# Flamingo layer pair, first attention: units of two heads on one batch instead of one head on one batch

## The reference

```python
x = x + tanh(g_xattn[0]) * xattn(layernorm(x), ctx, Wq, Wk, Wv, Wo, q_norm_w, k_norm_w)
# xattn: 32 query heads, 8 key/value heads (4 query heads each), head size 128
kv = concatenate([context, latents], axis=1)          # 512 + 256 = 768 keys per batch, 2 batches
q, k, v = latents @ Wq, kv @ Wk, kv @ Wv              # 256 queries per batch
q, k = rms_norm(q), rms_norm(k)                       # per head
probs = softmax(q @ k.T / sqrt(128))
out = (probs @ v).reshape(...) @ Wo
```

## Time and profile before

| | us |
|---|---|
| median of 3 runs (989.22 to 989.53) | 989.34 |
| the profiled execution | 990.12 |
| its span, first to last instruction | 988.3 |
| PE matmuls busy | 948.9 (96%) |
| DVE, ACT, POOL busy | 636.9, 479.9, 358.6 |

### The profile page before, as it was taken

One profiled execution on the slowest core, in us unless ns is written; L12 is line 12 of the kernel. 1 busy time (PEld: TensorE's weight loads), 2 busy tenths in 40 slices (PEclk: granted clock), 3 DMA queues, 4 the chain that ended last, 5 costly groups with the idle time before them and its releaser, 6 DMA issues. The chain is left out here.

```text
span 988.3 us, 18532 instructions
## 1 busy us (share of the span) xinstructions
PE 948.9 (96%) x6876; PEld 824.1 (83%) x6876; DVE 636.9 (64%) x1102; ACT 479.9 (49%) x937; POOL 358.6 (36%) x255
## 2 busy tenths in 40 slices
PE   4989999999999999999999999999999998999996
PEld 3969988998999899899989988998987886677755
DVE  5577547646765674576567557646754666888856
ACT  4356336534643563365356336534624612665634
POOL 3435316333341443253336317233214721080033
PEclk9999999999999999999999999999999999999999
DMA  6021203200310211032021103300006213933001
GB/s 234 1 49 49 55 1 85 55 9 1 94 53 0 74 25 49 0 85 64 0 60 36 53 0 85 73 12 4 30 15 221 85 43 123 223 73 60 2 1 43
DMA packets 40677, 55.01 MB, mean 56 GB/s; under 512 B 8640, under 2 KB 20544, under 8 KB 40640
## 3 DMA queue, kind: packets, MB, share of 16 engines
q1 hardware_dynamic: 40064, 54.49, 20.4%
q10 hardware_dynamic: 576, 0.00, 0.0%
HBM read 50.22 MB, written 4.26 MB: 55 GB/s over the span
## 5 line engine op out<-in xcount | busy, mean ns | idle before, releaser
L437 DVE TENSOR_TENSOR ptL<-tbank,ptH 128x512 fp32r<-128x512 f32 x192 | 132.3, 689 | 69.4 <-ACT ptH L306 66.8
L306 ACT ACTIVATE ptH<-tbank 128x512 fp32r<-128x512 f32 x192 | 115.7, 603 | 110.5 <-PE tbank L553 110.2
L553 PE MATMUL tbank<-ident,probs 128*128 128x128 f32 x864 | 132.5, 276 | 6.5 <-DVE ptL L437 3.3
L450 DVE TENSOR_REDUCE negmax<-score 128x1 f32<-128x768 f32 x128 | 120.5, 951 | 9.6 <-PE score L80 9.1
L327 ACT ACTIVATE probs<-score,negmax 128x768 f32<-128x768 f32 x128 | 115.7, 904 | 17.4 <-DVE negmax L450 17.3
L78 PE MATMUL obank<-ptH,vH 128*128 128x256 f32 x384 | 121.3, 316 | 0.0
L408 DVE TENSOR_REDUCE sumsq<-probs 128x2 f32<-128x256 f32 (+1 forms) x80 | 42.0, 526 | 114.9 <-ACT probs L301 71.8
L553 PEld LDWEIGHTS tbank<-ident,probs 128*128 128x128 f32 x864 | 97.5, 140 | 17.3 <-DVE ptL L437 10.3
L216 POOL TENSOR_TENSOR rnorm<-sumsq,neg_half 128x2 f32<-128x2 f32 (+1 forms) x80 | 71.4, 896 | 107.3 <-DVE sumsq L410 107.1
L80 PE MATMUL obank<-ptH,vL 128*128 128x256 f32 x384 | 108.8, 283 | 0.0
L80 PE MATMUL score<-wkvH,kvT_lo 128*128 128x256 f32 x384 | 108.7, 283 | 0.0
(11 more groups left out here) (263 smaller groups left out, 2233.7 us busy)
## 6 DMA issues: line engine op xcount, KB each, us to landing
wqo_stage<-in_wq SPq DMA_DIRECT2D x9, 1024.0 KB, 5.8
wqo_stage<-in_wo SPq DMA_DIRECT2D x8, 1024.0 KB, 7.2
factors<-r_scratch SPq DMA_DIRECT2D x32, 256.0 KB, 3.9
wkv_stage<-in_wkv SPq DMA_DIRECT2D x9, 512.0 KB, 6.6
a_qS<-q_scratch SPq DMA_DIRECT2D x24, 128.0 KB, 5.2
ctx_stage<-in_ctxT SPq DMA_DIRECT2D x2, 1024.0 KB, 12.8
kS<-k_scratch SPq DMA_DIRECT2D x32, 64.0 KB, 4.2
q_scratch<-qpart SPq DMA_DIRECT2D x16, 128.0 KB, 1.9
```

The source lines that it names most:

```text
L306: act.activation(out, tbank[c % 2][:], ACT.Copy, scale=scale).then_inc(t_hi, 1)
L437: i = dve.tensor_tensor(out, tbank[c % 2][:], f32(hi), ALU.subtract)
L450: dve.tensor_reduce(negmax[:, m:m + 1], score[m % 2][:, 0:SKV], AX.X, ALU.max, negate=True).then_inc(s_max, 1)
L553: i = pe.transpose(tbank[c % 2][:, n * P:(n + 1) * P], block_in, S.ident[:])
```

## The change

A unit w is now a pair of heads on one batch: heads 2(w // 2) and 2(w // 2)+1 on batch w % 2, four units per group. A unit has four score tiles and six chunks; a chunk is one key tile by the 512 query columns of both heads, so a V chunk is three matmuls of 512 columns into the whole `obank`. PE goes through the six chunks of a unit; behind each transposed chunk comes the V chunk that is two behind, and behind each of the first four a score tile of the next unit. `probs` has eight slots, ptH and ptL have three, the turned queries of two heads are kept, and heads 2 and 3 are turned within the second unit. Queries 0 and 1 and all four score tiles of the first unit are now made in the part between the groups (and ahead of the loop for group 0); `k_rows` and `sq` move to the second half of `probs`. `normalise_o` and the split of its result now run on two heads of one batch, and the output projection of the last group goes by batch. POOL splits Wo after score tile 5 instead of 3.

```diff
-    NP, NPT = 4, 4
+    NP, NPT = 8, 3
+    later = 4 * SKV
+    k_rows = probs_mem[:, later:later + NKT * D0].rearrange("p (t d) -> p t d", d=D0)
...
-    U, CH = 2 * GRP, 3
-    order = [("q", 0), ("k", 0), ("k", 1), ("k", 2)]
+    PAIRS, CH = GRP, KVT
+    order = [("q", 0), ("k", 0), ("q", 1), ("k", 1), ("k", 2)]
+    for w in range(PAIRS):
+        for j in range(CH):
+            if w == 1 and j < 2:
+                order.append(("q", 2 + j))
+            order.append(("p", CH * w + j))
...  # ACT
             def attend(g):
+                for w in range(PAIRS):
+                    if w == 1:
+                        hi_q(g, 2)
+                    hi_p(g, CH * w)
+                    if w == 1:
+                        hi_q(g, 3)
+                    for t in range(4):
+                        hi_p(g, CH * w + t + 1)
+                        if w + 1 < PAIRS:
+                            exp(g, 4 * w + 4 + t)
+                        if t == 1 and w:
+                            hi_o(g, w - 1)
+                    hi_p(g, CH * w + CH - 1)
+            def prepare(g):
+                for i in range(2):
+                    hi_q(g, i)
+                    hi_k(g, i)
                 exp(g, 0)
+                hi_k(g, 2)
+                for m in range(1, 4):
+                    exp(g, m)
...  # DVE
             def attend(g):
+                for w in range(PAIRS):
+                    reciprocals(g, w)
+                    if w == 1:
+                        lo_q(g, 2)
+                    lo_p(g, CH * w)
+                    for t in range(4):
+                        if w + 1 < PAIRS:
+                            maximum(g, 4 * w + 4 + t)
+                        if w == 1 and t == 0:
+                            lo_q(g, 3)
+                        lo_p(g, CH * w + t + 1)
+                        if w and t == 0:
+                            normalise_o(g, w - 1)
+                    lo_p(g, CH * w + CH - 1)
...  # PE
+            def transpose_probs(g, w, j):
                 if j == 0:
+                    pe.wait_ge(s_exp, 16 * g + 4 * w + 4)
+            def times_v(g, c):
+                w, j = c // CH, c % CH
+                if j == 0 and w >= 2:
+                    pe.wait_ge(o_normed, GRP * g + w - 1)
                 pe.wait_ge(t_lo, TC * g + at["p", c] + 1)
+                key = (w % 2) * KVT + j
+                mm3(pe, obank[w % 2][:], (vH[:, key, :], vL[:, key, :]), (ptH[:, c % NPT, :], ptL[:, c % NPT, :]),
+                    j == 0, j == CH - 1).then_inc(pe_pv, 1)
             def attend(g):
+                for w in range(PAIRS):
+                    if w == 1:
+                        transpose_q(g, 2)
+                    for j in range(CH):
+                        if w == 1 and j == 1:
+                            transpose_q(g, 3)
+                        transpose_probs(g, w, j)
+                        if CH * w + j >= 2:
+                            times_v(g, CH * w + j - 2)
+                        if j < 4 and w + 1 < PAIRS:
+                            scores(g, w + 1, j)
...  # PE, ahead of the loop
-            transpose_q(0, 0)
-            for i in range(3):
-                transpose_k(0, i)
-            scores(0, 0)
+            for t in range(2):
+                transpose_q(0, t)
+                transpose_k(0, t)
+            scores(0, 0, 0)
+            scores(0, 0, 1)
+            transpose_k(0, 2)
+            scores(0, 0, 2)
+            scores(0, 0, 3)
```

More of the change, by code:

```diff
@@ L466, in normalise_o, with lo_p @@
                                   ALU.mult).then_inc(o_normed, 1)
+            def lo_p(g, c):
+                lo(g, ("p", c), ptL[:, c % NPT, :], ptH[:, c % NPT, :])
             def attend(g):
[L469 to L485, removed]
+                for w in range(PAIRS):
[12 more added lines that the diff above has]
+                    lo_p(g, CH * w + CH - 1)
             def add_out(g, t, bank):
@@ L499, in turn @@
                 add_out(g, 0, obank[0][:])
+                lo_q(g + 1, 1)
                 lo_k(g + 1, 1)
                 add_out(g, 1, obank[1][:])
+                maximum(g + 1, 0)
                 lo_k(g + 1, 2)
-                maximum(g + 1, 0)
-                maximum(g + 1, 1)
+                for m in range(1, 4):
+                    maximum(g + 1, m)
                 add_out(g, 2, obank[0][:])
@@ L514, in _ @@
             fill_items(0, 0)
-            lo_q(0, 0)
-            for i in range(3):
+            for i in range(2):
+                lo_q(0, i)
                 lo_k(0, i)
             maximum(0, 0)
-            maximum(0, 1)
+            lo_k(0, 2)
+            for m in range(1, 4):
+                maximum(0, m)
             turns(dve, turn, last)
@@ L563, in transpose_q, with scores @@
                 transposes(g, ("q", h), [q_rows[:, t, h * D0:(h + 1) * D0] for t in range(RT)])
-            def scores(g, u, tiles=(0, 1)):
-                h, b = u // 2, u % 2
-                if b == 0 and h:
+            def scores(g, w, t):
+                hp, b, m = w // 2, w % 2, 4 * w + t
+                h = 2 * hp + t // 2
+                if b == 0:
                     pe.wait_ge(t_lo, TC * g + at["q", h] + 1)
-                if h == 0:
+                if hp == 0:
                     pe.wait_ge(t_lo, TC * g + at["k", 1 + b] + 1)
[L571 to L579, removed]
@@ L600, in attend @@
-            def attend(g):
[L602 to L610, removed]
-                    for j in range(CH):
-                        if u == U - 1:
-                            times_v(g, u - 1, j)
-                        if u or j:
-                            transpose_probs(g, u, j)
-                        if 0 < u < U - 1:
-                            times_v(g, u - 1, j)
+                if m >= 2:
+                    pe.wait_ge(s_exp, 16 * g + m - 1)
@@ new lines, in scores @@
+                q = slice(b * SQ + (m % 2) * P, b * SQ + (m % 2 + 1) * P)
+                for k0, n in ((0, 512), (512, 256)):
+                    keys = slice(b * SKV + k0, b * SKV + k0 + n)
+                    i = mm3(pe, score[m % 2][:, k0:k0 + n], (qTH[:, h % 2, q], qTL[:, h % 2, q]),
+                            (kTH[:, keys], kTL[:, keys]), True, True)
+                i.then_inc(pe_s, 1)
+            def transpose_probs(g, w, j):
+                if j == 0:
+                    pe.wait_ge(s_exp, 16 * g + 4 * w + 4)
+                transposes(g, ("p", CH * w + j),
+                           [probs[:, (4 * w + n) % NP, j * P:(j + 1) * P] for n in range(4)])
@@ L641, in turn @@
                 project_kv(g + 1)
[L642 to L648 removed]
+                for t in range(2):
+                    transpose_q(g + 1, t)
+                    transpose_k(g + 1, t)
+                    output(g, t)
+                scores(g + 1, 0, 0)
+                scores(g + 1, 0, 1)
+                transpose_k(g + 1, 2)
+                output(g, 2)
+                scores(g + 1, 0, 2)
+                scores(g + 1, 0, 3)
+                output(g, 3)
             def output_heads(t, heads):
```

81 lines of the change are left out of this document (20 added, 61 removed).

## The result

| | before | after |
|---|---|---|
| median of the runs, us | 990.61 (12 runs) | 992.68 (12 runs) |
| the profiled execution | 990.12 | 993.13 |
| its span | 988.3 | 991.2 |
| start of group 0 | 18.58 | 18.40 |
| group 0 | 83.73 | 90.82 |

The changed kernel is slower by 2.1 us: its time is 1.0027 of before, 95% interval 1.0018 to 1.0036. Forecast was 985.3, the range ended at 990.5. A group starts with its first query projection; the table goes from one such start to the next.

The account below looks back on a forecast made before the run. PE was taken to bound the eight groups, with only 1.7 us of waits in a group's attention. Terms 3.3 + 0.2 - 3.5 - 4.0 = -4.0 gave a median of 985.3 us, range 979.5 to 990.5.

Parts of the forecast that it names:

- the head's chain: Ahead of the loop: four score tiles and no chunk done at 65.7, against six and three before; 3.3 us lost.
- the head's clock: Ahead of the loop: 1.2 GHz until 56.6 as before, nothing added for the clock.
- V in 512 columns: V products: 576 matmuls of 512 columns replace 1152 of 256, at the output projection's 0.2333 us each; 4.0 us won.
- waits in the groups: PE's waits in attention: 1.1 to 1.2 us instead of 1.7; 3.5 us won over groups 1 to 7, group 0 loses 0.2.
- the second rival: Ahead of the loop: new waits keep the clock at 1.2 GHz until 65.7; 988.3 us, no change; chance 0.13.
- end of 8 for the head: Ahead of the loop: upper end of the forecast loss, 8 us, if the clock stays low.
- the first border: Between units 0 and 1: head 2's queries take a `tbank`, so PE waits 0.7 us ahead of a later chunk.
- the last unit: Last unit of a group, no scores: normalisation delays the low part and oTH; 0.4 us of waits including restarts.
- the second and third border: Between units 1 and 2, and 2 and 3: chunk 5's low part just met, normalisation caught up; 0 wait.
- the first rival: Unit borders: late normalisation on DVE makes PE wait 0.45 us at 16 borders; 7.2 us lost, 992.5; chance 0.13.
- The third rival: V products: a 512-column matmul costs 0.240 us, so nothing is won; 989.3 us, no change; chance 0.10.
- The end: Behind the last V chunk: PE has 5.6 us of output work ahead of the first matmul needing it; 0.

Follow-up runs that it names:

- experiments 1 and 2: Unread 512-column matmuls put in PE's waits ahead of the loop: 33 in the changed kernel, 989.23 us; 12 in the kernel before, 988.97 us.
- experiment 4: Changed kernel with V matmuls of 256 columns again, except the first and last pass of a unit's sum: 993.63 us, ratio 1.0036.
- experiment 9: Changed kernel with head 2's queries turned earlier, third key block and third unit's normalisation later, two k/v projections in the head's waits: 976.94 us, ratio 0.9859.

## Why the prediction was wrong

| term | forecast | measured | from |
|---|---|---|---|
| the head's chain | +3.3 | +3.9 | experiments 1 and 2, full clock |
| the head's clock | 0 | +3.2 | 4.2 after less 0.96 before |
| V in 512 columns | -4.0 | -3.3 | 17 ns by 192 chunks |
| waits in the groups | -3.3 | -0.4 | 1.86 a group to 1.78; group 0 0.4 more |
| ahead of the head, behind the groups | 0 | -0.6 | -1.1 and +0.5 in the two traces; scatter, see below |
| sum | -4.0 | +2.8 | by the spans +2.9 (988.3 to 991.2) |

- **The clock of the head is the step that failed.** The prediction kept the grant "at 1.2 GHz until 56.6 as before" and full from there. It had a row with the opposite (a wait of 2.8 us, then a grant of 0.58), and it had put three more waits of 0.7 to 2 us into the new head; it gave the second rival 0.13. The rival's mechanism came true, at another place: not until 65.7 but from 64.7, 1.0 us into the wait of 2.16, and over the chunks and score tiles that follow, which the forecast had left at their full-clock prices. Its end of 8 for the head was near the 3.9 + 3.2 measured. Experiments 1 and 2 show it by filling the waits and leaving the chain; what the stretches cost came to 4.2 us, against 0.96 before.
- **The head's chain** was followed step by step and holds to 0.1 us at the first chunk (65.77 for 65.7). That needed luck: the last k/v projection matmul came 1.1 us earlier than before (47.43 for 48.52), and without that the chunk would have been as much later, since 1.2 GHz lasted until 57.8 and not 56.6. From that matmul on the chain is 3.9 longer at full clock and not 3.3.
- **The waits in the groups were mis-sized.** The waits that were named are there: 0.72 at the first border, 0.40 with restarts in the last unit. At the second and third border the forecast was 0, by a margin of 0.03; there is none, and PE waits 0.05 for the exponential, some 0.1 with the restart. That is the first rival's mechanism, and its sign of being wrong, at under a quarter of the 0.45 that it gave. The sum of 1.1 to 1.2 also left out what was not looked for: 0.30 at the doubled transposes of queries and keys behind the output row tiles (0.13 before) and 0.10 at the third score tile. That made 1.78 and not 1.15, and before it was 1.86 and not 1.7: of 0.5 won per group 0.1 is left.
- **V in 512 columns** has the spacing of the nearest row (0.231 to 0.235 for 0.233). What it replaced was 0.118 to 0.121 apart and not always 0.120, so the term is 3.3. And a term on PE inside a group does not reach the time whole: in experiment 4 only 0.18 of 0.34 us per group did. The third rival (no gain from the width) is wrong, though its 989.3 was nearer to the measured time than the forecast.
- **The end** cost nothing on the path, as forecast: 36 matmuls stand behind the last V chunk in both kernels, 24 of them ahead of the first that needs its result. Group 7 is 1.43 shorter where the others are 0.51 shorter; 0.7 of the rest only changes sides: two V chunks instead of three stand behind a group's boundary, so group 0 counts one more and group 7 one less.

What stands ahead of the head moved the last k/v projection matmul 1.1 us forward, and the traces say by what. Group 0's query projections begin at 1.2 GHz in every trace (the granted clock in the windows reads 1.00 there, but the matmuls of 512 columns start 0.43 apart and then 0.23). Before, with the low clock until 22.5:

```profile
21.71 0.63 PE L79 MATMUL score<-wqL,kvT_hi 128*128 128x512 f32 x1
...
22.76 0.39 PE L79 MATMUL score<-wqL,kvT_hi 128*128 128x512 f32 x1
```

and after, until 20.3:

```profile
19.40 0.63 PE L80 MATMUL score<-wqH,kvT_lo 128*128 128x512 f32 x1
...
20.50 0.39 PE L80 MATMUL score<-wqH,kvT_lo 128*128 128x512 f32 x1
```

From group 0's start the low clock lasts 3.9 us before and 1.9 after, and the last k/v projection matmul comes 29.94 and 29.03 us behind that start. In the other eight traces in which PE's matmuls up to there have this order, the low clock lasts between 2.0 and 5.2 us and the distance goes with it, from 29.06 to 30.55, half a microsecond for one. So 0.9 of the -1.1 (the rest is group 0's earlier start) is luck of the profiled execution and no gain of the change; what decides how long the clock stays low there was not tried. What lies behind the groups, the +0.5, is scatter too (248.9 to 251.9 us in the twelve traces). And the medians differ by 2.1 us where the profiled spans differ by 2.9 because the profiled execution of before is 0.5 under its median and that of after 0.45 over; the forecast is wrong by either.

## What to carry to other kernels

Where a change lengthens a chain of waits on PE, price it twice: once for the wait, and once for what PE does behind it at 1.2 GHz, by the rows in which the profile already shows a lowered grant behind a wait. When work is taken from between two stages, put independent real work into the gap that it leaves; here two projections moved into it, with the clock held at full, took some 3.7 us off the first group. Before comparing two traces, look for stretches at 1.2 GHz outside the part in question, since they move spans by a microsecond or more from one execution to the next. Count a group's waits from start spacings over the whole group, not from the places one has thought of.

## What the runs showed that I had not expected

- In the head the clock fell within or just behind waits of PE of 2 to 3 us: 0.7 us behind the end of one of 2.80 (before), 0.3 ahead of the end of one of 2.70 and 1.0 us into one of 2.16 (after), 0.2 behind one of 2.33 (experiment 9). Adding 33 matmuls that nothing reads made the kernel 4.3 us shorter in span.
- The first matmul behind transposes takes 0.31 to 0.32 to the next start, for 0.23 otherwise, at 512 columns; at 256 it takes 0.20 for 0.12. The surcharge of 0.08 is the same, so it is paid once per chunk either way.
- Every wait of PE ahead of transposes cost 0.056 us beyond itself here (their rows show 0.66 for 0.60), so many small waits cost more than their sum.
